# Both self-attentions: turned probabilities ahead, output per tile, softmax sums by products with ones; the second MLP product by tile

## The reference, cut to what matters

```python
# self-attention: 16 heads of 32, causal, within each sequence of 64
s = where(causal, q @ k.T / sqrt(32), masked)       # 64 x 64 per head and sequence
p = exp(s - max(s)) / sum(exp(s - max(s)))           # softmax over the keys
x = x + (p @ v) @ wo                                 # layer 0: with biases; layer 1: rotary, one key/value head
# second layer's MLP, 2048 hidden
h = gelu(layernorm_out @ W1 + b1)
out = x + layernorm(t + h @ W2 + b2) * g_norm_out + b_norm_out
```

## Time and profile before

| what | us |
|---|---|
| median of 3 runs | 2342.01 |
| lowest and highest of them | 2341.47, 2346.83 |
| the profiled execution: time | 2339.05 |
| its span, first to last instruction | 2337.3 |
| TensorE busy | 2116.4 |
| VectorE busy | 1002.1 |
| ScalarE busy | 700.4 |
| stage b in that span | 877 to 973 |
| last product of the MLP, and stage e | 1836 to 1891, 1905 to 1978 |

### The profile page before, as it was taken

One profiled execution on the slowest core, in us unless ns is written; L12 is line 12 of the kernel. 1 busy time (PEld: TensorE's weight loads), 2 busy tenths in 40 slices (PEclk: granted clock), 3 DMA queues, 4 the chain that ended last, 5 costly groups with the idle time before them and its releaser, 6 DMA issues. The chain is left out here.

```text
span 2337.3 us, 26028 instructions
## 1 busy us (share of the span) xinstructions
PE 2116.4 (91%) x9802; PEld 1232.6 (53%) x9802; DVE 1002.1 (43%) x2019; ACT 700.4 (30%) x1382; POOL 408.7 (17%) x468
## 2 busy tenths in 40 slices
PE   7989999999999898899999997778599976899999
PEld 3545555555555544444444443333233434899998
DVE  6455655656556404310000016999753055412120
ACT  2444544444445311321111114455302112111111
POOL 0000000000000001089988511222100000000010
PEclk9999999999999998799999998998799988899999
DMA  6102121221221314378887747342240100766652
GB/s 216 41 20 83 38 75 45 69 82 46 76 66 42 120 39 163 106 301 307 317 311 301 291 167 258 127 169 78 81 184 19 42 9 26 291 236 230 238 211 78
DMA packets 130925, 327.12 MB, mean 140 GB/s; under 512 B 39617, under 2 KB 88801, under 8 KB 111474
## 3 DMA queue, kind: packets, MB, share of 16 engines
q1 hardware_dynamic: 98368, 293.59, 35.0%
q10 hardware_dynamic: 29730, 23.29, 3.1%
q0 software_dynamic: 2704, 8.59, 1.1%
HBM read 303.40 MB, written 20.91 MB: 139 GB/s over the span
## 5 line engine op out<-in xcount | busy, mean ns | idle before, releaser
L876 PE MATMUL a_mix<-a_xn,a_probs_T 128*128 128x384 f32 (+1 forms) x832 | 311.6, 491 | 14.4 <-issue 9.4
L805 PE MATMUL a_sc<-a_wk_centred,a_ctx_T 128*128 128x512 f32 x624 | 288.2, 599 | 2.3 <-DVE a_keys L463 2.3
L1879 PE MATMUL c_gate_up<-bc_w_wide,c_h_rows 128*128 128x512 f32 x480 | 210.9, 592 | 0.0
L876 PEld LDWEIGHTS a_mix<-a_xn,a_probs_T 128*128 128x128 f32 (+1 forms) x832 | 145.2, 190 | 119.5 <-issue 71.5
L805 PEld LDWEIGHTS a_sc<-a_wk_centred,a_ctx_T 128*128 128x128 f32 x624 | 117.8, 192 | 125.6 <-issue 105.0
L1783 DVE TENSOR_TENSOR c_hidden<-c_silu,c_gate_up 128x512 f32<-128x512 f32 x38 | 26.1, 688 | 360.9 <-PE c_gate_up L1879 355.0
L1879 PEld LDWEIGHTS c_gate_up<-bc_w_wide,c_h_rows 128*128 128x128 f32 x480 | 90.2, 190 | 108.0 <-issue 108.0
L2334 PE MATMUL f_ring<-f_picked_T,f_w 128*128 128x160 f32 x1024 | 143.5, 300 | 0.0
L2349 PE MATMUL f_ring<-f_hidden,f_w 128*128 128x160 f32 x1024 | 141.4, 300 | 1.5 <-ACT f_hidden L2224 1.5
L2349 PEld LDWEIGHTS f_ring<-f_hidden,f_w 128*128 128x128 f32 x1024 | 139.3, 190 | 2.1 <-ACT f_hidden L2224 1.8
L2334 PEld LDWEIGHTS f_ring<-f_picked_T,f_w 128*128 128x128 f32 x1024 | 139.9, 190 | 0.2
(11 more groups left out here) (535 smaller groups left out, 3233.6 us busy)
## 6 DMA issues: line engine op xcount, KB each, us to landing
bc_w_wide<-in_L_ffn_W SPq DMA_DIRECT2D x64, 1024.0 KB, 5.9
f_w<-in_L_ffn_W SPq DMA_DIRECT2D x32, 2048.0 KB, 8.9
c_w_down<-in_L_ffn_W SPq DMA_DIRECT2D x34, 1024.0 KB, 7.3
a_ctx_T<-in_ctx_T SPq DMA_DIRECT2D x48, 384.0 KB, 3.5
a_xn<-in_ctx SPq DMA_DIRECT2D x24, 768.0 KB, 7.2
d_context<-in_ctx SPq DMA_DIRECT2D x8, 2304.0 KB
d_context_T<-in_ctx_T SPq DMA_DIRECT2D x12, 768.0 KB, 7.0
cd_context_T<-in_ctx_T SPq DMA_DIRECT2D x9, 768.0 KB, 7.7
```

Of the source, the lines that this page charges most:

```text
L805: last = pe.matmul(key_bank(b, t), ctx_T[:, n % AHEAD, k, cols], wk_centred[:, k, :], start=(k == 0), stop=(k == KC - 1))
L876: ins = pe.matmul(mix[:, 0:DC], probs_T[0:m, t, p * P:(p + 1) * P], xn[0:m, b % 2, t, :], start=(t == 0), stop=(t == CT - 1))
L1879: last = pe.matmul(gate_up[2 * (u % 2) + part][:], h[:, k, :], w_wide[:, i % WIDE_RING, k, :], start=(k == 0), stop=(k == KD - 1))
```

## The change

In `causal_attention`:

- The ring's uses are written out as a list, `uses`, and each bank has its own pair of semaphores. `place`, `wait_full`, `wait_out`, `wait_free`, `full` and `out` look a use up by name. In the new order of uses the output projection of a tile, ("y", t - 1), stands between the turned probabilities of tile t and the outputs of tile t.
- The exponentials are turned and multiplied undivided. Beside each of the 32 value products of a tile stands a second product of the same turned exponentials with a 64x32 tile of ones. It fills a second half of the output's bank with the softmax sum, repeated over the 32 rows of the head.
- VectorE divides at the end: two reciprocals of 128x256 from PSUM and two multiplications of 128x256 from PSUM into `o_T`, for each tile. The row sum, the small reciprocal, the 128x1024 multiplication (L1254, L1256, L1258) and ScalarE's copy to `o_T` (L1342) are gone.
- `project` and `end_tile` run per tile.

In `film_and_mlp`: the first quarter is taken for all tiles, and then quarters two to four of tile 0, of tile 1, and so on. VectorE does all of a tile before the next, and `ROOTS` is put in that order.

```diff
-        R_TILE = R_V + NT
-        R_Y = R_TILE + 4 * NT
+        if rope:
+            late = [("value", t) for t in range(NT)]
+        else:
+            late = [("value", 0), ("value", 1)]
+        for t in range(NT):
+            late += [("turned", t, j) for j in range(2)]
+            if not rope and t < 2:
+                late.append(("value", 2 + t))
+            if t:
+                late.append(("y", t - 1))
+            late += [("o", t, cp) for cp in range(2)]
+        late.append(("y", NT - 1))
+        uses = [("hT", t) for t in range(NT)] + [("proj", n) for n in range(NPROJ)] + late
+        use_of = {what: u for u, what in enumerate(uses)}
+
+        def place(*what):
+            return ring[use_of[what] % 4]
...
+        def wait_out(eng, *what):
+            u = use_of[what]
+            eng.wait_ge(ring_out[u % 4], u // 4 + 1)
+
+        def wait_free(eng, *what):
+            u = use_of[what]
+            if u >= 4:
+                eng.wait_ge(ring_out[u % 4], u // 4)
...
             def divide(t):
-                dve.wait_ge(exped, t + 1)
-                own.did(dve.tensor_reduce(total[:, t, :], scores[:, t, :, :], AXX, ALU.add))
-                own.wait()
-                own.did(dve.reciprocal(total[:, t, :], total[:, t, :]))
-                own.wait()
-                dve.tensor_tensor(scores[:, t, :, :], scores[:, t, :, :],
-                                  total[:, t, :].unsqueeze(2).to_broadcast([P, H, SEQ]),
-                                  ALU.mult).then_inc(probs_ready, 1)
...
+                for cp in range(2):
+                    wait_full(dve, "o", t, cp)
+                for cp in range(2):
+                    own.did(dve.reciprocal(inverse[:, cp], place("o", t, cp)[:, 2:4, :]))
+                own.wait()
+                for cp in range(2):
+                    own.did(dve.tensor_tensor(o_T[:, cp::2, t * P:(t + 1) * P], place("o", t, cp)[:, 0:2, :],
+                                              inverse[:, cp], ALU.mult))
+                own.wait()
+                for cp in range(2):
+                    dve.sem_inc(out("o", t, cp), 1)
+
+            def end_tile(t):
+                if t == 0 and not rope:
+                    dve.wait_ge(biased, 1)
+                wait_full(dve, "y", t)
+                own.did(dve.tensor_tensor(g.x[:, t, :], flat(place("y", t)), g.x[:, t, :], ALU.add))
+                own.wait()
+                dve.sem_inc(out("y", t), 1)
...
+            for t in range(NT if rope else 0):
+                put_values(t)
+            centre(0)
+            centre(1)
+            for t in range(0 if rope else 2):
+                put_values(t)
+            centre(2)
             if not rope:
+                put_values(2)
+            centre(3)
+            divide(0)
+            if not rope:
+                put_values(3)
+            divide(1)
+            end_tile(0)
+            divide(2)
+            end_tile(1)
+            normalize(0)
+            divide(3)
+            for t in range(2, NT):
+                end_tile(t)
+                normalize(t - 1)
             normalize(NT - 1)
 
...
+            def put_turned(t):
+                if t >= 2:
+                    wait_full(act, "o", t - 2, 1)
+                for j in range(2):
+                    wait_full(act, "turned", t, j)
+                    act.activation(probs_T[:, t % 2, 4 * j:4 * j + 4, :], place("turned", t, j)[:],
+                                   ACT.Copy).then_inc(out("turned", t, j), 1)
...
+            def turn(t):
+                pe.wait_ge(exped, t + 1)
                 for j in range(2):
+                    wait_free(pe, "turned", t, j)
...
+            def outputs(t):
+                for j in range(2):
+                    wait_out(pe, "turned", t, j)
+                for cp in range(2):
+                    wait_free(pe, "o", t, cp)
                 pe.wait_ge(v_moved[t], 32)
+                last = [None, None]
                 for half_c in range(2):
                     for i in range(4):
                         for b in range(2):
...
+                                source = v if cp == b else v_swapped
+                                shares = probs_T[at, t % 2, 2 * i + half_c, tok]
+                                pe.matmul(place("o", t, cp)[i * HD:(i + 1) * HD, half_c, tok],
+                                          source[at, t, cols], shares, start=True, stop=True)
+                                last[cp] = pe.matmul(place("o", t, cp)[i * HD:(i + 1) * HD, 2 + half_c, tok],
+                                                     ones[at, :], shares, start=True, stop=True)
+                for cp in range(2):
+                    last[cp].then_inc(full("o", t, cp), 1)
+
+            def project(t):
+                if t == 0:
+                    pe.wait_ge(o_in, 16)
+                for cp in range(2):
+                    wait_out(pe, "o", t, cp)
+                wait_free(pe, "y", t)
+                for k in range(KD):
+                    last = pe.matmul(flat(place("y", t)), o_T[:, k, t * P:(t + 1) * P], wo[:, k, :],
+                                     start=(k == 0), stop=(k == KD - 1))
+                last.then_inc(full("y", t), 1)
+
+            if rope:
+                for t in range(NT):
+                    values(t)
+            pe.wait_ge(heads_ready, NQK)
+            pe.wait_ge(rows_made, 8)
+            pe.wait_ge(ones_made, 1)
+            pair_scores(0)
+            if not rope:
+                values(0)
+                values(1)
+            pair_scores(1)
+            for t in range(NT):
+                turn(t)
+                if not rope and t < 2:
+                    values(2 + t)
+                if t:
+                    project(t - 1)
+                outputs(t)
+            project(NT - 1)
...
-            for i in range(NT + 2):
-                if i < NT:
-                    add_hidden(i)
-                if 0 <= i - 1 < NT:
-                    end_tile(i - 1)
-                if 0 <= i - 2 < NT:
-                    normalize(2, i - 2, g.x[:, i - 2, :], g.hn[:, i - 2, :])
+            for t in range(NT):
+                add_hidden(t)
+                end_tile(t)
+                normalize(2, t, g.x[:, t, :], g.hn[:, t, :])
...
-            for q in range(4):
+
+            def down(t, q):
                 pe.wait_ge(down_in[q], 16)
                 pe.wait_ge(wide_out, (q + 1) * KD)
...
+                for k in range(KD):
+                    m = q * KD + k
+                    last = pe.matmul(y[t][:], hidden[:, m, t * P:(t + 1) * P], w_down[q][:, k, :],
+                                     start=(m == 0), stop=(m == FC - 1))
+                if q == 3:
+                    last.then_inc(y_full, 1)
+
+            for t in range(NT):
+                down(t, 0)
+            for t in range(NT):
+                for q in range(1, 4):
+                    down(t, q)
```

More of the change, by code:

```diff
@@ L1146, in causal_attention @@
         zeroed, mask_made, rows_made = s.sem("zeroed"), s.sem("mask_made"), s.sem("rows_made")
-        ring_full, ring_out = s.sem("ring_full"), s.sem("ring_out")
+        ring_full = [s.sem(f"ring_full{i}") for i in range(4)]
+        ring_out = [s.sem(f"ring_out{i}") for i in range(4)]
         heads_ready = s.sem("heads_ready")
@@ L1211, in _ @@
                 for n in range(NQK):
[L1213 to L1216, removed]
+                    wait_full(dve, "proj", n)
+                    own.did(dve.stream_shuffle(half[:], flat(place("proj", n)), SWAP_HALVES))
+                    own.did(dve.tensor_tensor(qk_T[:, n, :], flat(place("proj", n)), cos[:], ALU.mult))
                     own.wait()
-                    dve.sem_inc(ring_out, 1)
+                    dve.sem_inc(out("proj", n), 1)
                     own.did(dve.tensor_tensor(half[:], half[:], sin[:], ALU.mult))
@@ L1224, in _ @@
                 for n in range(NQK):
-                    u = R_PROJ + n
-                    dve.wait_ge(ring_full, u + 1)
-                    own.did(dve.tensor_scalar(qk_T[:, n, :], flat(ring[u % 4]), bias[:, n:n + 1], None, ALU.add))
+                    wait_full(dve, "proj", n)
+                    own.did(dve.tensor_scalar(qk_T[:, n, :], flat(place("proj", n)), bias[:, n:n + 1], None, ALU.add))
                     own.wait()
-                    dve.sem_inc(ring_out, 1)
+                    dve.sem_inc(out("proj", n), 1)
+                    dve.sem_inc(heads_ready, 1)
             def put_values(t):
-                u = R_V + t
-                dve.wait_ge(ring_full, u + 1)
-                part = flat(ring[u % 4])[:, 0:v_cols]
+                wait_full(dve, "value", t)
+                part = flat(place("value", t))[:, 0:v_cols]
                 if rope:
@@ L1238, in put_values @@
                 own.wait()
-                dve.sem_inc(ring_out, 1)
+                dve.sem_inc(out("value", t), 1)
                 dve.sem_inc(v_ready, 1)
@@ L1445, in _ @@
+            project(NT - 1)
```

(9 more changed lines are left out.)

136 lines of the change are left out of this document (34 added, 102 removed).

## The result

| | before | changed |
|---|---|---|
| median | 2341.74 | 2384.28 |
| lowest and highest (4 runs each) | 2338.72, 2346.83 | 2381.11, 2385.03 |
| the profiled execution: time | 2339.05 | 2385.03 |
| its span | 2337.3 | 2383.3 |

The ratio is 1.018, interval 1.0161 to 1.02: the change makes the kernel slower. 2376 had been forecast.

A forecast was written before the change was run, and what follows sets the result against it. TensorE, busy 91% of the span at nearly full clock, was taken as the bound. Stage b +11.4, stage e +12.3, MLP's end -6.6 and clock +16.8 summed to +33.9 us, a median of 2376, range 2357 to 2393.

The forecast's parts named there:

- that chain: Attention stages b and e: division, addition, half a turn, projection and outputs in series; b +11.4 us, e +12.3 us.
- The signs listed ahead: Stages b and e: eight 1.75 us reciprocals each, TensorE idle some 4 us, clock about 0.7, additions 11 to 14 us apart.
- The MLP's end: VectorE's tail after the MLP's last product: 6.3 us in place of 12.9, so -6.6 us (bounds -7.0 to -6.2).
- The division: VectorE in stages b and e, between outputs and projection: 4.4 us a tile against 2.7 before, with reciprocals of 1.75 us.
- the bound of 0.43: Lower bound in us for a 128x256 reciprocal on VectorE, if it cost as an addition does; 1.75 was taken.
- rival 3: Attention's reciprocals from PSUM cost no more than an addition, so the kernel is not slower: 2338 us; chance 0.05.
- The small products: TensorE in b and e: a tile's value products and products with ones take 2.1 us, bounds 1.05 and 5.7.
- Rival 2: Products with ones don't overlap the value products, 5.7 us a tile instead of 2.1, giving 2398 us; chance 0.12.
- The clock: TensorE in b and e: eight projections behind pauses start at half clock, 2.1 us each, +16.8 us (bounds 0 to 27.4).
- Rival 1: TensorE's clock holds in the pauses of b and e, leaving +17.1 us alone: 2359 us; chance 0.15.
- starts at 1.1 to 3.4 us: Range of cost for each of eight half-clock projection starts in b and e, given as 2366 to 2387 us.
- The rounds at full clock: One tile's round in b and e: addition 0.7, half a turn 0.55, projection 3.43, outputs 2.1, divide 4.4; 11.2 us.

The follow-up runs named there:

- e4: Changed kernel with a tile's outputs placed ahead of the previous tile's projection on TensorE and in the ring's uses; 2354.14 us, ratio 1.0049.
- e6: Changed kernel with outputs ahead of the projection, eight wide products with ones, and outputs of tiles 1 to 3 in the scores' banks; 2334.41 us, ratio 0.9956.
- e1: The MLP part of the change alone, with the attention of the kernel before; 2333.58 us, ratio 0.997.
- e2: Changed kernel with each 128x256 reciprocal cut to 128x16 and the other inverses a constant 1, all waits kept; 2343.47 us, ratio 1.0002.
- e5: Changed kernel with a tile's 32 products with ones of 64 columns made eight of 256 columns, behind the value products; 2374.5 us, ratio 1.0133.
- e3: Changed kernel with TensorE's pauses filled by 4 or 5 products of 128x512 that nobody reads; 2363.25 us, ratio 1.0098.
- e7: Changed kernel with the early division of the kernel before, projection per tile kept, VectorE's and ScalarE's lists reordered; 2325.56 us, ratio 0.992.
- e8: Early-division kernel with per-tile projection, plus VectorE reordered: additions before the first normalisation, and in stage e an earlier division of tile 1; 2317.53 us, ratio 0.9888.

## Why the prediction was right, and where it was off

**Direction and mechanism.** Slower by the series of division, addition, half a turn, projection and outputs: that chain is in the trace link by link, and both experiments that break it where the prediction put it took most of the loss away: of the 48.5 us that b and e had lost, the order alone (e4) gave back 30, and order, banks and fewer products together (e6) 45. The signs listed ahead came out in kind: eight reciprocals of 1.7 us in each stage, TensorE idle 4.8 us with the addition as what ends it, a clock of about 0.75. Two went a little past what was said: the rounds' additions are 13.9 to 14.4 us apart (11 to 14), and b and e are longer by 23 and 25 us (17 to 22).

**The MLP's end.** -6.6 forecast, -6.57 in the pair of traces, 6.4 us of tail in e1.

**The division.** 4.4 us a tile forecast; in the round above it is 4.48 from the reciprocals' start to the addition's. 1.75 was right for a reciprocal from PSUM; the bound of 0.43 is far off, and with it rival 3. e2 shows that even shorter ones, 0.37 a pair, would have ended at 2343 and not below the kernel before.

**The small products.** This term was too small: 2.1 us for a tile's outputs, measured 2.6 (966.8 to 969.4 in the windows), on the path about six times, so 3 us. Rival 2, 5.7 us, is out by the same row; e5, with a quarter as many products with ones, gained 1 us a tile.

**The clock.** 16.8 us forecast, as eight starts at 2.1 us. Two experiments give it apart from the rest: 40.8 - 24.0 = 17 (e2, where one projection was still slow), and 17.4 in the stretches of e3, 19.1 without its slow first outputs. By rows, the eight groups of four 128x512 products behind pauses (seven projections and b's `values(3)`; b's first projection came behind that and at full clock) were longer than 3.60 by 1.6 to 3.0 us, 17.8 together, and four half turns by 0.45 each: 19.6. So the term was right in kind and some 2 to 3 us low, because the half turn in front ran at half clock as well and some projections for longer. Rival 1, that the clock holds, fell: 2363 in e3 is where such a kernel ended. By the prediction's own numbers, starts at 1.1 to 3.4 us give 2368 to 2386, not 2366 to 2387; the measured 2384 lies near the upper end.

**The rest.** The rounds at full clock are 11.9 us in e3 where 11.2 was forecast; 0.5 of it is the outputs', and 0.2 is left for hand-overs. Changed stretches measured +41.9 against +33.9: about 3 the clock, 3 the small products, and 2 that are left, hand-overs in all likelihood. The remaining 4 us between the profiled executions lie outside these stretches. Two terms were thus mis-sized by some 3 us each, the small products (2.1 us for a tile's outputs, 2.6 measured) and the clock's price; none was of the wrong sign.

**What the prediction did not see.** It named the old order's back to back projections as the cover that is lost, but not how much of the loss comes from the ring, which ties the tiles together: with the outputs ahead, fewer and in other banks (e6) b and e are within 2.3 and 0.9 us of before. Which of the three does most in e6 was not taken apart beyond e4 and e5. The late division stays the worse one even so. Held against e7, which has the projection per tile as well but divides early, e6 is longer by 11.2 us in b and 5.3 in e, and a round is 6.9 to 7.4 us in b instead of 5.4.

## What to carry to other kernels

Before work is moved behind the product that feeds it, write down one full round over all engines: if the new order leaves a single chain through two engines, the round is the sum, and TensorE's pause can be charged again in its clock (here 1.6 to 3.0 us behind each pause of 3.7 to 4.8). Projection and additions per tile were worth having here with the early division (13 us in b and e together, e7); the late division was not, and the two came in one change, so try such parts one by one. A reciprocal is paid by the element on VectorE (0.25 us for 128x16, 1.73 for 128x256): invert a sum once, before it is spread over columns.

## What the runs showed of the hardware

- TensorE's clock. Pauses of 3.7 to 4.8 us were followed by half clock each time in the changed kernel, eight of eight. Pauses of 1.6 to 1.8 us (e2) were in one case of six. Close to each other, a pause of 1.95 us ahead of a projection in e6 was followed by half clock (5.29 us for it) and one of 1.84 in e8 was not (3.67). Filling the pauses with products that nobody reads saved 17 us in the stretches and 21 in the median.
- TensorE can stand still without a semaphore to wait for: 1.3 to 1.9 us inside a run of 128 small records, in four of the eight runs of e4, those of tiles 2 and 3 in each stage, which had no long pause before them. The same 128 records ran through in 2.5 us in the changed kernel with its pauses of 4.8 us, and also in e2, where the pauses are 1.6 to 1.8 us; e6, with 80 records a tile, has no such stall either. What holds TensorE there was not tested, and the cause stays open.
- Twice as many small products on the same places cost 2.4 times as much: 64 products in 2.5 us, 20 ns a record, against 16 ns before.
